# Attention with row scores left in PSUM: two buffers for row tiles and one for pairs in place of a shared ring of three

## The reference

```python
xn = layernorm(x)                                  # over the 512 features
# attention, 16 heads of 32
q, k, v = xn @ Wq.T, xn @ Wk.T, xn @ Wv.T
attn = softmax(q @ k.T * 512**-0.5)                # per head, 1024 x 1024
attn = attn + bias_table[i - j + S - 1]            # bias is added AFTER the softmax
s = layernorm(attn @ v) * ln_gamma + ln_beta
# feed-forward with a spiking gate
y = (relu(xn @ W_fc.T) ** 2) @ W_proj.T
g = silu(number of spikes of a 5-step neuron driven by y / 5)
out = x + s * g
```

## Time and profile before

| | |
|---|---|
| median of 3 runs | 3607.78 us (3604.3 to 3609.36) |
| profiled execution | 3608.45 us |
| its span | 3606.7 us |
| main slots, from the first pair matmul to the last | 1460.8 to 3567.3 us |
| PE busy share of the span | 96% |
| ACT | 73% |
| DVE | 68% |
| POOL | 44% |

### The profile page before, as it was taken

One profiled execution on the slowest core, in us unless ns is written; L12 is line 12 of the kernel. 1 busy time (PEld: TensorE's weight loads), 2 busy tenths in 40 slices (PEclk: granted clock), 3 DMA queues, 4 the chain that ended last, 5 costly groups with the idle time before them and its releaser, 6 DMA issues.

```text
span 3606.7 us, 55124 instructions
## 1 busy us (share of the span) xinstructions
PE 3449.5 (96%) x19961; PEld 1448.1 (40%) x19964; DVE 2434.5 (68%) x3950; ACT 2632.5 (73%) x3928; POOL 1570.2 (44%) x897
## 2 busy tenths in 40 slices
PE   6999999999999998999999999999999999999984
PEld 2444444444444443343433433433434334334331
DVE  5554444445455544777888888788788788788786
ACT  5333333333333334999999999999999999999994
POOL 0000000000000000576776776777777777867777
PEclk8999999999999998999999999999999999999997
DMA  4111211221111112231332232322322222233221
GB/s 177 45 56 56 79 56 57 80 67 54 54 54 56 56 39 76 60 101 42 96 111 77 81 103 77 100 83 82 95 83 88 90 91 85 84 100 99 61 77 65
DMA packets 220318, 278.78 MB, mean 77 GB/s; under 512 B 96112, under 2 KB 131696, under 8 KB 219536
## 3 DMA queue, kind: packets, MB, share of 16 engines
q1 hardware_dynamic: 220048, 275.26, 25.0%
HBM read 157.87 MB, written 59.83 MB: 60 GB/s over the span
## 4 chain that ended last, share of the span: by engine, by line
ACT 35%; issue 10%; PE 8%; DVE 5%; DMA 1%; SPq 1%; POOL 1%; ACTq 0%; DVEq 0%; POOLq 0%
ACT recurrence_or_probs L1161 19%; ACT s_sb L1168 17%; PE misc L1035 2%; DVE s_sb L1235 2%; PE s_ps L1081 2%; PE acc L1112 2%; PE s_ps L1095 2%; DVE gate_or_tokens L1323 1%; POOL recurrence_or_probs L1428 1%; DMA xT<-xnT 1%; SPq L961 1%; DVE nat L1271 0%; DVE outT L1254 0%; PE misc L1017 0%; DVE frs L1313 0%
## 5 line engine op out<-in xcount | busy, mean ns | idle before, releaser
L1235 DVE TENSOR_SCALAR_CACHE_REDUCE s_sb<-s_ps 128x1024 f32<-128x1024 f32 x1024 | 1243.8, 1221 | 383.3 <-PE s_ps L1081 348.7
L1428 POOL TENSOR_TENSOR recurrence_or_probs<-recurrence_or_probs,toep 128x2048 f32<-128x2048 f32 (+3 forms) x384 | 1321.6, 3460 | 275.3 <-ACT recurrence_or_probs L1161 275.3
L1168 ACT ACTIVATE s_sb<-s_sb,nmax 128x1024 f32<-128x1024 f32 x1024 | 1195.2, 1167 | 13.5 <-DVE s_sb L1235 13.4
L1161 ACT ACTIVATE recurrence_or_probs<-s_ps 128x1024 f32<-128x1024 f32 x1024 | 1058.6, 1035 | 17.0 <-PE s_ps L1095 16.8
L354 PE MATMUL ps_fc<-xnT_part,w_fc 128*128 128x512 f16 x3072 | 710.4, 381 | 17.9 <-DVE w_fc L544 10.5
L369 PE MATMUL ps_y<-w_pr,hid_part 128*128 128x512 f16 x3072 | 707.0, 380 | 3.5 <-DVE w_pr L544 3.5
L480 ACT ACTIVATE relu<-ps_fc 128x512 f32<-128x512 f32 x256 | 152.8, 597 | 719.8 <-PE ps_fc L354 719.8
L1081 PE MATMUL s_ps<-kst,qst 96*128 96x512 f16 x2048 | 615.9, 382 | 56.7 <-ACT recurrence_or_probs L1161 43.7
L633 DVE TENSOR_TENSOR hid<-relu 128x512 f32<-128x512 f32 x256 | 177.0, 692 | 684.4 <-ACT relu L480 684.4
L1095 PE MATMUL s_ps<-qst,kst 99*128 99x512 f16 x2048 | 615.6, 383 | 2.3 <-DMA qst<-sub_rows 0.7
L1463 POOL MEMSET unit<- 128x16 f32 x1 | 0.1, 111 | 1388.8 <-POOLq L145 1388.8
(11 more groups left out here) (141 smaller groups left out, 2204.3 us busy)
## 6 DMA issues: line engine op xcount, KB each, us to landing
toep<-table_rows SPq DMA_DIRECT2D x32, 2048.0 KB, 8.3
qst<-nat SPq DMA_DIRECT2D x384, 64.0 KB, 2.0
kst<-nat SPq DMA_DIRECT2D x384, 64.0 KB, 2.0
x_in<-in_x SPq DMA_DIRECT2D x16, 1024.0 KB, 8.6
xnT<-xnT_part SPq DMA_DIRECT2D x32, 512.0 KB, 5.8
gate<-gate_or_tokens SPq DMA_DIRECT2D x16, 1024.0 KB, 4.4
xT<-xnT SPq DMA_DIRECT2D x32, 512.0 KB, 9.8
x_or_gate<-gate SPq DMA_DIRECT2D x64, 256.0 KB, 2.9
```

The lines of the kernel that those rows point to most:

```text
L1161: nc.scalar.activation(prob[:, k % PROBS, 2 * second:2 * second + 2, :].rearrange("p j n -> p (j n)"), s_ps[:, item_buffer(pair_item(m)), ...
L1168: nc.scalar.activation(s_sb[:, i % 4, :], s_sb[:, i % 4, :], ACT.Exp, bias=nmax[:, par, j, st:st + 1], scale=-1.0, accum_out=den[:, par, j ...
L1235: nc.vector.tensor_scalar(s_sb[:, i % 4, :], s_ps[:, item_buffer(tile_item(n)), :], -1.0, None, ALU.mult, ALU.min, accum_out=nmax[:, par, ...
L1428: nc.gpsimd.tensor_tensor(tile, tile, toep[:, par, :, at:at + width], ALU.add).then_inc(biased, 1)
```

## The change

The copy `s_sb` is gone. `row_max` is now a reduction that writes the negated maximum only; `exp_sum` reads the row tile in PSUM and writes its unneeded exponentials as bf16 to `sink`. The six banks are dealt out anew: row tiles alternate between two buffers of two banks, and pairs have one buffer of two banks, `st_ps`. A row tile's buffer is now released by `exp_sum` (`sum_done`), a pair's by the `exp_pair` just before it. The order of work in every queue stays as it was.

```diff
-        s_sb = sb("s_sb", [P, 4, S], F32)
+        sink = sb("sink", [P, 2, S], BF16)
-        s_ps = pt("s_ps", [P, RING, S], F32)
+        s_ps = pt("s_ps", [P, 2, S], F32)
+        st_ps = pt("st_ps", [P, S], F32)
 def prelude_bank(n):
-            return (s_ps[:, RING - 1, :BANK], 1, spiking.xT_first) if n % 2 else (misc, 0, spiking.xT_first)
+            return (st_ps[:, :BANK], 1, spiking.xT_first) if n % 2 else (misc, 0, spiking.xT_first)
 def score_tile(G, par, i):
-                x = tile_item(n)
-                if item_release(x):
-                    pe.wait_ge(*item_release(x))
+                wait(pe, sum_done, n - 1)
...
-                    last = nc.tensor.matmul(s_ps[:, item_buffer(x), c * 512:(c + 1) * 512], ...
+                    last = nc.tensor.matmul(s_ps[:, i % 2, c * 512:(c + 1) * 512], ...
 def score_pair(s, k, second):
-                if item_release(x):
-                    pe.wait_ge(*item_release(x))
+                wait(pe, p_done, m)
...
-                    last = nc.tensor.matmul(s_ps[:, item_buffer(x), i * 512:(i + 1) * 512],
+                    last = nc.tensor.matmul(st_ps[:, i * 512:(i + 1) * 512],
 def exp_pair(s, k, second):
-                                     s_ps[:, item_buffer(pair_item(m)), :], ACT.Exp).then_inc(p_done, 1)
+                                     st_ps[:], ACT.Exp).then_inc(p_done, 1)
 def exp_sum(G, par, i):
                 act.wait_ge(max_done, n + 1)
-                nc.scalar.activation(s_sb[:, i % 4, :], s_sb[:, i % 4, :], ACT.Exp, bias=nmax[:, par, j, st:st + 1], scale=-1.0,
+                wait(act, sum_done, n - 1)
+                nc.scalar.activation(sink[:, i % 2, :], s_ps[:, i % 2, :], ACT.Exp, bias=nmax[:, par, j, st:st + 1],
                                      accum_out=den[:, par, j, st:st + 1]).then_inc(sum_done, 1)
 def row_max(G, par, i):
                 dve.wait_ge(s_done, n + 1)
-                wait(dve, sum_done, n - 3)
-                nc.vector.tensor_scalar(s_sb[:, i % 4, :], s_ps[:, item_buffer(tile_item(n)), :], -1.0, None, ALU.mult, ALU.min,
-                                        accum_out=nmax[:, par, j, st:st + 1]).then_inc(max_done, 1)
+                nc.vector.tensor_reduce(nmax[:, par, j, st:st + 1], s_ps[:, i % 2, :], AX, ALU.max, negate=True).then_inc(max_done, 1)
```

More of the change, by code:

```diff
@@ L715 @@
 PROBS = 4
-RING = 3
-AHEAD = 2 * (SLOT_STEPS - TILE_LAG)
 def attention(nc, d, w, spiking, NB):
@@ L856, in before @@
             return (b, hg - 1) if hg else (b - 1, 3)
[L858 to L885, removed]
         def bias_width(k):
@@ L1076, in score_tile @@
                     pe.wait_ge(stacked[j], G * 96 + 96)
-                x = tile_item(n)
-                if item_release(x):
-                    pe.wait_ge(*item_release(x))
+                wait(pe, sum_done, n - 1)
                 for c in range(2):
-                    last = nc.tensor.matmul(s_ps[:, item_buffer(x), c * 512:(c + 1) * 512], qst[0:ROWS, par, j, st * P:(st + 1) * P],
+                    last = nc.tensor.matmul(s_ps[:, i % 2, c * 512:(c + 1) * 512], qst[0:ROWS, par, j, st * P:(st + 1) * P],
                                             kst[0:ROWS, par, j, c * 512:(c + 1) * 512], start=True, stop=True)
@@ L1085, in score_pair @@
             def score_pair(s, k, second):
-                x = pair_item(s.g * 32 + 2 * k + second)
+                m = s.g * 32 + 2 * k + second
                 half, tb = k // 8, k % 8
```

## The result

The changed kernel takes 3826.04 us (median of 3 runs, 3825.91 to 3827.24) against 3607.78. The ratio is 1.061, 95% interval 1.0591 to 1.0629. The forecast was 3807, with a range of 3715 to 3885.

What follows compares the result with a forecast made beforehand. PE's 4.13 us for two half-steps, with ACT's 4.06 close to it, was taken as the bound. 174 + 6 + 1.5 + 4 + 3 + 11 = 199.5 us more gave 3807 us, range 3715 to 3885.

Steps and rivals of the forecast that it cites:

- The loop: Main slots: `exp_pair`, `exp_sum`'s release, row tile, projection, pair, next `exp_pair`; 4.55 us per two half-steps against 4.13.
- The present turn: Kernel before, two half-steps in main slots: PE's work taken as 4.13 us, ACT's as 4.06.
- The bound on the exponential's gain: `exp_sum` reading PSUM: at most 0.13 us shorter, 0.03 taken.
- The slot: 16 turns (two half-steps each) with q/k projections sum to 72.02 us against 66.21; +174 us over thirty slots.
- 0.4 for VectorE: Eviction and normalisation together (h = 18 to 23) not quite covered: 0.4 us in each of 28 slots, +11 us.
- The row maximum as a reduction: `row_max` without its 1024-column write: 1.22 us taken, 0.9 to 1.37 kept as bounds.
- The rival in which VectorE becomes the bound: Evictions meet row maxima in phase, slack of 1.3 us used up: +78, 3885 us; chance 0.10.
- The pair's single buffer: `score_pair` waits for `exp_pair`: 1.69 us, hidden behind ACT's 2.03 per half-step while row tiles run.
- The clock: TensorE's granted clock: no fall expected; rival of 1.2 GHz everywhere, some 1300 us more, chance 0.02.
- Early release: Row tile released with `exp_sum`'s ACTIVATE, not its readout, exponential 0.13 shorter: turn 4.23, about 3680 us; chance 0.06.
- faster: `exp_sum` as cheap as `exp_pair`, row tile's wait over before PE comes: 3565 us; chance 0.03.
- no change: Row tile's release 0.42 us earlier, just reached by early release and shorter exponential together: 3608 us; chance 0.02.

Runs made afterwards that it cites:

- e3: The changed kernel with PE's order in main slots turned: pair, then projection or weighing, then row tile; 3801.71 us, ratio 1.0537.
- e7: The changed kernel with projection or sum ahead of the row tile in even half-steps only; 3800.86 us, ratio 1.0536.
- e9: e7 without the second of VectorE's two instructions that take q and k out of PSUM (low parts zero); 3747.07 us, ratio 1.0387.
- e1: The changed kernel's new banks with the old row maximum that copies to SBUF, row tiles released by the maximum; 3627.17 us, ratio 1.0053.
- e4: The changed kernel with one of the seven accumulating products of `sum_values` kept; 3795.18 us, ratio 1.0519.
- e10: e7 with the old order (row tile first) again at h = 28 and 30; 3800.51 us, ratio 1.0535.

## Why the prediction was right, and what it missed

*The loop* was right in mechanism and size: release 2.18 us after `exp_pair` (2.19 forecast), turn 4.55 (4.55), bubble ahead of even tiles only, v turns 4.59 (4.60), the turn of `sum_values` without a fall of the clock 4.73 (4.75). Undoing the hold together with the missing copy gave back 199 of 218 us, shortening the hold by the readout 49. The present turn was put at PE's 4.13; in the trace before it is ACT's 4.07 at nearly every place, PE lagging in half-steps with projections and catching up in others. The forecast does not hang on it, for it takes the slot of today from the trace, 66.21. The bound on the exponential's gain held too: `exp_sum`'s ACTIVATE fell from 1.167 to 1.115 us on average, but its readout starts only 0.04 earlier.

*The slot*: 72.02 + 0.4 for VectorE was forecast; slots without a dip take 72.43 on average, against 66.21 before. The 72.02 is earned turn by turn, the agreement to 0.01 is luck: the 0.4 for VectorE (11 us of the sum) is not there. All 14 waits of ACT for a row maximum lie before 1465 us, in the prelude, none in a main slot. The 0.4 is filled by small things that the prediction did not count: in every second slot from the second batch on ACT's two small instructions for the normalisation's root, which put 0.35 us into the turn around h = 10 (4.35 for 4.00), the two turns with transposes (8.55 for 8.40), and 0.07 us in each of the turns around h = 6, 14 and 18.

*The row maximum as a reduction* takes 1.222 us, what was taken between the bounds of the earlier trace rows. ACT waited for it for only 14 us in all, against 13 in the kernel before. The rival in which VectorE becomes the bound fell for this order of the queue; with PE's order turned VectorE's evictions did take the gain, as e3, e7 and e9 show.

*The pair's single buffer* was called hidden; the new banks by themselves cost 18 us (e1), and PE's longest wait there is on this buffer. That the longer loop covers it in the changed kernel is inferred from the turns, which came out without such a term.

*The clock* was the largest term that was mis-sized. The prediction expected no fall, because PE at 81% busy had kept 1.00, and priced only a fall everywhere. What happened is small falls in 11 of 30 slots, 15 us, within 7 us behind the 8-column matmuls that follow a bubble. That is most of the 18.8 us by which 218.3 exceeds the 199.5 forecast. The rule of the Trainium skill that stood beside this rival ("TensorE: Matmul & The Clock Gate", the section on the second failure mode: brief idling while cycling PSUM banks can make the clock oscillate) agrees with this trace only in part: PE waits for a PSUM buffer in nearly every turn, and the clock fell only behind `sum_values`. The rest is small: the first `exp_pair` comes 4.5 us later where 3 were forecast, and the last two slots cost 11.1 us where 11.5 were forecast.

*Early release, faster, no change*: none came. The release waits for the readout's end (2525.05 to 2525.11), so the first did not occur.

What stays open: why a dip follows `sum_values` in some slots and not in others. e4 and e10 together point to both the short matmuls and the wait just ahead of them: without most of the former (e4) or with the wait moved behind them (e10) there is none. Both runs shift the work around them as well, so how the two act together is not shown.

## What to carry to other kernels

Removing a copy out of PSUM lengthens the time for which its buffer is held by all that the last reader waits for and does. Follow the release to the instruction that waits for it, add what is queued behind that on the same engine until the chain comes back to the reader, and compare with the present period: here 2.19 + 1.73 + 0.63 = 4.55 against 4.13, from rows of the old trace alone. When a forecast comes out to 0.01, look at its terms one by one all the same: one of them was not there. Moving work ahead of a wait shortens such a loop only as far as that work's own buffer is emptied in time; check that bank's eviction before expecting the gain.

## What the runs showed of the hardware

What an instruction costs depends on the loop in which it stands: the readout left out takes 213 us of rows off ACT and 49 us off the kernel. An exponential of 1024 columns with its sum takes 1.115 us from PSUM to bf16 against 1.167 from SBUF to fp32, in place, and its readout starts 0.04 earlier; source and destination changed together, so neither has a price of its own. A row maximum of 1024 columns takes 1.222 us as a plain reduction and 1.221 with the full copy written beside it. In the changed kernel TensorE's granted clock kept 1.00 through turns with a wait of 0.2 to 0.3 us of the matmuls ahead of projections, and fell, in the middle of attention, only within some 7 us behind matmuls of 8 columns with such a wait ahead of them.
